# Four-layer attention and mixture-of-experts kernel: third expert stage with destinations inside the rows, next weights issued by ScalarE, and the last group of the third attention normed by VectorE

## What is computed

```python
x = x + _L0_xattn_ref(ctx_1024, _layernorm(x), ...); x = x + _L0_ffn_ref(_layernorm(x), ...)
x = x + _L1_xattn_ref(_layernorm(x), ctx_1024, ...); x = x + _L1_ffn_ref(_layernorm(x), ...)
x = x + _L2_xattn_ref(ctx_1024, _layernorm(x), ...); x = x + _L2_ffn_ref(_layernorm(x), ...)
x = x + _L3_xattn_ref(_layernorm(x), ctx_1024, ctx_1024, ...); x = x + _L3_ffn_ref(_layernorm(x), ...)
```

```python
def _L2_ffn_ref(x, gate_w, gate_up_w, down_w):
    router_probs = jax.nn.softmax(x_flat @ gate_w, axis=-1)
    top_k_probs, top_k_idx = jax.lax.top_k(router_probs, TOP_K)      # TOP_K = 2
    top_k_probs = top_k_probs / jnp.sum(top_k_probs, axis=-1, keepdims=True)
    gate_up = jnp.einsum('nd,edh->enh', x_flat, gate_up_w)
    hidden = jax.nn.silu(gate_up[..., :F]) * gate_up[..., F:]
    expert_out = jnp.einsum('enf,efd->end', hidden, down_w)
    ...   # each row takes the outputs of its two experts, weighted
```

## Time and profile before

| | |
|---|---|
| median of 3 runs | 1934.75 us (1924.11 to 1939.05) |
| profiled execution, its own time | 1931.34 us |
| its span, first to last instruction | 1929.6 us |
| mean granted TensorE clock | 0.854 |
| busy: PE, DVE, ACT, POOL | 77%, 61%, 43%, 40% of the span |
| third attention, its loop and what surrounds it | about 674 to 1479 us |
| third expert stage | about 1479 to 1634 us |

### The profile page before, as it was taken

The page is one execution under the profiler, slowest core; times in us unless marked ns, Lnnn a source line. Parts: engine busy times, 40 slices in busy tenths (PEclk is TensorE's granted clock), DMA queues, the critical chain, the costliest instruction groups (busy, mean ns, idle before and its releaser), DMA issues. The chain is left out here.

```text
span 1929.6 us, 36666 instructions
## 1 busy us (share of the span) xinstructions
PE 1489.4 (77%) x10502; PEld 1341.8 (70%) x10503; DVE 1176.5 (61%) x3742; ACT 821.3 (43%) x2527; POOL 777.7 (40%) x769
## 2 busy tenths in 40 slices
PE   6776999336576659999999999999983796463773
PEld 4555999225456549999999999999973685243773
DVE  4556444127866437778787878787863464767223
ACT  4443555102122136666666666666641222341331
POOL 2012442650001545555656556565543454001662
PEclk8776999655666769999999999999995898775986
DMA  9203222110012120000000000000002422102113
GB/s 188 1 0 116 76 65 55 49 41 1 1 44 73 36 88 12 12 2 15 10 16 7 15 7 18 4 7 4 11 8 74 123 73 73 56 1 61 42 41 105
DMA packets 90308, 78.57 MB, mean 41 GB/s; under 512 B 16196, under 2 KB 77351, under 8 KB 90087
## 3 DMA queue, kind: packets, MB, share of 16 engines
q1 hardware_dynamic: 71432, 49.20, 10.2%
q0 software_dynamic: 12160, 24.99, 4.3%
q10 hardware_dynamic: 6624, 3.28, 0.6%
HBM read 50.86 MB, written 27.10 MB: 40 GB/s over the span
## 5 line engine op out<-in xcount | busy, mean ns | idle before, releaser
L1800 POOL TENSOR_TENSOR paired_rows<-paired_rows,rinv 128x1024 f32<-128x1024 f32 x128 | 242.6, 1895 | 282.8 <-DVE rinv L2106 279.8
L1963 ACT ACTIVATE paired_rows<-psum_banks,neg_max 128x256 f32<-128x256 f32 x512 | 237.4, 490 | 0.6 <-DVE neg_max L2111 0.6
L2097 DVE TENSOR_TENSOR probs_turned_lo<-psum_banks,probs_turned_hi 128x512 fp32r<-128x512 f32 x256 | 175.7, 686 | 96.4 <-ACT probs_turned_hi L1945 82.5
L1851 PE MATMUL psum_banks<-y_turned_parts,queries_hi 128*128 128x256 f32 x1024 | 201.0, 294 | 3.0 <-DVEq L1701 3.0
L1886 PE MATMUL psum_banks<-probs_turned_hi,y_rows 128*128 128x512 f32 x512 | 192.0, 416 | 0.4 <-issue 0.4
L1945 ACT CAST probs_turned_hi<-psum_banks 128x512 fp32r<-128x512 f32 x256 | 151.1, 590 | 57.4 <-PE psum_banks L1835 55.0
L1835 PE MATMUL psum_banks<-ident,paired_rows 128*128 128x128 f32 x1024 | 155.4, 274 | 8.3 <-DVEq L1701 3.0
L1851 PEld LDWEIGHTS psum_banks<-y_turned_parts,queries_hi 128*128 128x128 f32 x1024 | 158.9, 192 | 3.5 <-issue 3.5
L2111 DVE TENSOR_REDUCE neg_max<-psum_banks 128x4 f32<-128x1024 f32 x128 | 156.0, 1219 | 7.1 <-PE psum_banks L1851 4.2
L1945 ACT CAST queries_hi<-psum_banks 128x512 fp32r<-128x512 f32 x128 | 75.0, 586 | 172.4 <-PE psum_banks L1874 169.1
L1851 PE MATMUL psum_banks<-y_turned_parts,queries_lo 128*128 128x256 f32 x512 | 145.0, 283 | 0.0
(11 more groups left out here) (747 smaller groups left out, 3465.3 us busy)
## 6 DMA issues: line engine op xcount, KB each, us to landing
normed_rows_dram<-paired_rows SPq DMA_DIRECT2D x3, 2048.0 KB, 8.7
tile_rows__<-rows_by_expert SPq DMA_DIRECT2D x71, 65.0 KB
expert_rows<-expert_rows_sb SPq DMA_DIRECT2D x71, 64.0 KB, 1.5
expert_w_b<-in_L_ffn_w_dram SPq DMA_DIRECT2D x2, 2048.0 KB
staged_pairs<-expert_rows SPq DMA_DIRECT2D x8, 512.0 KB
paired_rows<-expert_rows SPq DMA_DIRECT2D x8, 512.0 KB, 6.0
x_rows<-in_x_dram SPq DMA_DIRECT2D x8, 256.0 KB, 5.5
expert_w_a<-in_L_ffn_gate_up_w_dram SPq DMA_DIRECT2D x1, 2048.0 KB, 9.7
```

The costliest lines, as they stand in the source:

```text
L1800: ins = pool.tensor_tensor(probs[:, p, :, :], probs[:, p, :, :], rinv[:, p, :].unsqueeze(2).to_broadcast([P, 4, 256]), ALU.mult)
L1851: ins = pe.matmul(bank[S_BANKS[par] + h // 2][:, (h % 2) * 256:(h % 2 + 1) * 256], queries[q][:, h, :], yparts[:, 2 * s2 + y, :], start=(k ...
L1963: ins = act.activation(probs[:, par, h, :], bank[S_BANKS[par] + h // 2][:, (h % 2) * 256:(h % 2 + 1) * 256], ACT.Exp, bias=nmax[:, par, h: ...
L2097: ins = dve.tensor_tensor(lo, bank[bank_][:, :], hi.bitcast(F32), ALU.subtract)
```

## The change

- The rows in HBM are 129 words: 128 values and the destination itself, as an integer. For that each group's tail exists twice (`tails[0]`, `tails[1]`), one for each choice, with 2n and 2n+1 in the last word. ScalarE makes the second copy in `keep_tail`; the tiles lie in `Y1`, those of the last group in `XN`, no longer in `staged_pairs`.
- In the third expert stage VectorE no longer computes the destination; POOL's scatter reads it from the loaded tile. A tile load therefore waits until the slot's old tile has been scattered (`slot_is_free`).
- The fourth layer's weights are issued by ScalarE at the start of the third expert stage, before its table load and first Silu, and no longer by SP between the loads of tiles 7 and 8.
- The last group of the third attention: Ln and Exp on ScalarE, one refinement and the scalings on VectorE (four for each copy, the signal to TensorE after the first four). POOL no longer scales there. Its places have a buffer of their own.
- The paddings are split: experts 0 to 3 on SP's queue, 4 to 7 on ScalarE's. ScalarE's stand between `keep_tail` of the last group and the Exp for the mix weights.
- A table with Ln and Exp is loaded on ScalarE at the attention's start. The table of owners for all partitions goes; one partition's remains.

```diff
-        xb = nc.dram_tensor("rows_by_expert", [E * REGION + SPARE_TILES * P, P + 2], F32).ap()
+        xb = nc.dram_tensor("rows_by_expert", [E * REGION + SPARE_TILES * P, P + 1], F32).ap()
...
                     def load_tile(j, s):
                         if not isinstance(j, int) or j >= SLOTS:
-                            sp.wait_ge(rows_turned_kept.sem, j + (rows_turned_kept.value - SLOTS + 1))
+                            slot_is_free(sp, j, s)
...
-                    if layer in (0, 2):
+                    if layer == 0:
                         load_expert_weights(sp, layer + 1)
...
-                            pool.indirect_dma_start(ys, bass.IndirectOffsetOnAxis(ap=DEST[:, i:i + 1], axis=0), yo[:, i % SLOTS, :], None).then_inc(expert_out[i % SLOTS].sem, 16)
+                            to = xr[:, i % SLOTS, P:P + 1].bitcast(U32) if kept else DEST[:, i:i + 1]
+                            pool.indirect_dma_start(ys, bass.IndirectOffsetOnAxis(ap=to, axis=0), yo[:, i % SLOTS, :], None).then_inc(expert_out[i % SLOTS].sem, 16)
...
+                    if layer == 2:
+                        load_expert_weights(act, layer + 1)
                     run(act, step)
...
-                            if kept:
-                                dve.tensor_scalar(DEST[:, bass.ds(j, 1)], xr[:, s, P + 1:P + 2], tile_owner[:, bass.ds(j, 1)], xr[:, s, P:P + 1], ALU.not_equal, ALU.add)
                             dve.tensor_copy(xt[:, s % 2, :], bank[s % 2][:, 0:P]).then_inc(rows_turned_kept.sem, 1)
...
+                def place_pads(eng, experts_):
+                    eng.wait_ge(ends_known.sem, 1)
+                    for e in experts_:
+                        at_ = eng.value_load(pad_at[0:1, e:e + 1], min_val=0, max_val=E * REGION - P)
+                        eng.dma_start(xb[bass.ds(at_, P), :], pads_dram[e * P:(e + 1) * P, :]).then_inc(pads_placed.sem, 16)
...
-                            pool.indirect_dma_start(xb, bass.IndirectOffsetOnAxis(ap=spots[:, k, j:j + 1], axis=0), rows_of(n)[:, j, :], None).then_inc(rows_spread.sem, 16)
+                            pool.indirect_dma_start(xb, bass.IndirectOffsetOnAxis(ap=spots_of(n)[:, k, j:j + 1], axis=0), rows_of(n)[k][:, j, :], None).then_inc(rows_spread.sem, 16)
...
                     spread(NG - 2, range(2 * G))
-                    tail_part(NG - 1, 10)
                     spread(NG - 1, range(2 * G))
...
                 def keep_tail(act, n):
                     act.wait_ge(tail_turned_made.sem, n + 1)
+                    if not (isinstance(n, int) and n == NG - 1):
+                        act.copy(tails[1][:, :, 0:P], tails[0][:, :, 0:P])
                     act.copy(flat(tail_turned[:, :, :]), bank[Q_BANK][:, :]).then_inc(tail_kept.sem, 1)
...
-                        dve.tensor_scalar(rows_of(n)[:, :, P], row_number[:, bass.ds(n * G, G)], 2.0, None, ALU.mult)
-                        dve.tensor_copy(rows_of(n)[:, :, P + 1], ix[:, :, 0])
                         for k in range(2):
+                            dve.tensor_scalar(rows_of(n)[k].bitcast(U32)[:, :, P], row_number[:, bass.ds(n * G, G)], 2.0, float(k), ALU.mult, ALU.add)
...
                 @block.scalar
                 def _(act):
+                    act.preload_act_table_set("natural_log_exp_and_others")
                     keep_turned(act, 0, Q_BANK, context_turned, 0, 2)
...
                     all_steps(act_step)(act)
+                    act.wait_ge(spread_known.sem, spread_known.value + 1)
+                    act.activation(row_work[:, 2, G:2 * G], row_work[:, 0, G:2 * G], ACT.Ln, scale=-2.0)
+                    act.drain()
+                    act.activation(row_rstd[:, G:2 * G], row_work[:, 2, G:2 * G], ACT.Exp, scale=-0.5).then_inc(roots_made.sem, 1)
                     keep_tail(act, NG - 1)
+                    place_pads(act, range(E // 2, E))
                     act.wait_ge(leads_made.sem, 1)
...
                     aggregate(dve, ch, [1])
-                    seed(dve, ch)
-                    refine(dve, ch, 3)
-                    keep_scales(dve, ch, None, NG - 1)
+                    dve.tensor_scalar(row_work[:, 0, G:2 * G], row_mv[:, G:2 * G, 1], EPS, -0.5, ALU.add, ALU.mult).then_inc(spread_known.sem, 1)
+                    dve.wait_ge(roots_made.sem, roots_made.value + 1)
+                    refine(dve, ch, 1)
+                    for k in range(2):
+                        for j in range(G):
+                            ins = dve.tensor_scalar(last_tails[k][:, j, 0:P], x_tile(NG - 1)(j), row_mv[:, G + j, 0:1], row_rstd[:, G + j:G + j + 1], ALU.subtract, ALU.mult)
+                        if k == 0:
+                            ins.then_inc(tail_ready.sem, 1)
```

64 lines of the change are left out of this document (31 added, 33 removed).

## The result

| | before | changed |
|---|---|---|
| median of 20 runs | 1931.76 us | 1920.34 us |
| ratio of the changed kernel to before, with 95% interval | | 0.9946 (0.9930 to 0.9962) |
| profiled execution, its own time | 1931.34 us | 1927.02 us |
| its span, mean granted clock | 1929.6 us, 0.854 | 1925.3 us, 0.856 |

A forecast was written before the change was run, and what follows sets the result against it. It took TensorE to bound the attention loop, then an unfilled handover, a load-queue hole and late VectorE in the tile loop. Terms -9.0 - 9.2 - 9.0 + 3 - 1 = -25.2 took 1934.75 to 1909.5 us; range 1899 to 1926.

The forecast's parts named there:

- Handover: Third attention's end into the third expert stage: moving the scalings off POOL saves 9.0 us (7 to 10).
- Hole and half clock: Third expert stage's start: weights on ScalarE's queue remove TensorE's 9.76 us tile wait and 1.96 behind it, 11.7 us.
- Start: Third expert stage's first tiles: weights moving while they load cost 1.5 us (0 to 4.0).
- Slower release: Third expert stage: slots freed after the scatter instead of the turn cost 1.0 us at the start (0 to 2).
- The landing: Third expert stage: a scatter's data, with the signal, taken to land 1.5 us after its 0.97 us issue.
- Tile loop: Third expert stage: dropping VectorE's destination instruction saves 0.13 us a tile over 71 tiles, 9 us (0 to 16).
- nothing in the tile loop: Rival, third expert stage: the wait moves to ScalarE's gate and the start gives back more; 1924 us, chance 0.14.
- shut-out: Rival, third expert stage's start: weights block tile loads from either queue, costing 12 us; 1918.5 us, chance 0.28.
- Attention loop: Third attention: ScalarE's second copy makes TensorE wait 0.45 us in each of 7 groups, +3 us (0 to 4).
- Table: Third attention: preloading the table moves a 1.28 us load into idle time, -1 us (0 to 1.3).
- main path: Whole kernel: the queues share the DMA engines and all terms sum to 1909.5 us; chance 0.52.

The follow-up runs named there:

- weights_late: Changed kernel with the next layer's weights issued on ScalarE's queue behind the third tile's gate instead of ahead of the first; ratio to before 0.9964.
- dve_extra: Changed kernel with VectorE's old destination instruction put back in the third expert stage, its output not read, scatters kept; ratio to before 0.9948.
- weights_sp: Changed kernel with the next layer's weights back on SP's queue, behind the first eight tile loads; ratio to before 0.9967.

## Why the prediction was wrong

- *Handover, -9.0: right.* 2.61 us from the variance to the transposes. To SP's first load it is -10.3; that the rest comes from the paddings, which now end before POOL, is likely and not shown. Two blocks of spreads with 4.18 between, as written.
- *Hole and half clock, -11.7: right in size, wrong in reason, so the size was luck.* From the first to the eleventh tile 11.3 came back. But the step "If the two queues share the DMA engines freely, the 9.76 goes" failed. ScalarE's queue has the hole too if it is used at about the old moment (`weights_late`: TensorE waits 7.22, 9.99 from tile to tile; before 9.76 and 11.52). What took the hole away was that the weights now flow while the first tiles are on their way.
- *Start, +1.5: mis-sized, 4.6.* The bounds ended at 4.0, taken from the earlier trace rows, where the weights lay beside POOL's gathers, and 1.5 was taken because "later tiles are issued long before they are needed". But the first tile has nothing ahead of it. In eleven other runs with the weights issued first it took 6.5 to 7.6 us to the first tile, so it cost up to 5.6.
- *Slower release, +1.0: nothing, as long as no weights flow.* In `weights_late`, where they flow, a slow scatter delays the release; the runs don't say what share of the hole is due to that. The landing that the prediction had to guess (0.97 + 1.5) was about right: on the second kind it is 2.3 us from a scatter's issue in the median.
- *Tile loop, -9.0: wrong on the chips of the first kind, +1.1 (from the eleventh tile to the next block 123.6 to 127.1 us in seven profiles of this loop, 122.2 and 122.8 before, so 1 to 5 us more).* The failed step is reading: VectorE's wait ahead of the removed instruction was "issue", so VectorE was called the late one. `dve_extra` shows what that reading was worth: with the instruction back the time is the same (0.9948). What VectorE gave earlier, 0.2 us a pair, came back as a later signal: from the products to the late gate 1.35 us before, 1.54 now, the end pinned to POOL's scatter. The rival "nothing in the tile loop" had the right outcome, with ScalarE's gate as the place, and not the cause. It priced the whole at 1924, the start at its end; the result lies between it and the shut-out's 1918.5 (its own sum, 1934.75 - 16, gives 1918.75). Where signals are not late, on the second kind, the same edit is worth 0.07 us a tile, about half of the 0.13 taken.
- *Attention loop, +3: right,* 0.54 a group, 3.9 in all. *Table, -1:* -2.2.

Sum by the profile: -10.3 + 4.6 - 11.3 + 1.1 + 3.9 - 2.2 = -14.2, by the ratio -10.4 (7.3 to 13.5 less); the spread of the loop between profiles is enough for the difference. The measured 1920 lies inside the forecast's range, but the main path to 1909.5 was wrong. Of the 11 us that the profile's sum lies short of the forecast, the tile loop is 10.1 and the start 3.1. The shut-out rival (0.28) is half true: weights hold back what lies beside them from whatever queue they are issued, but they slow it, they don't shut it out: the first tile came after 6.6 us, not 15. On this the Trainium skill, "DMA: Bandwidth & Descriptors", section "Issuing engines are not separate DMA queues", is borne out by `weights_late` against `weights_sp` (0.9964 and 0.9967): with the weights at about the same moment, it made no difference from which engine they were issued.

## What to carry to other kernels

When a loop's slack is put down to one engine's "issue", compare two neighbouring turns of the loop first. Here the same instruction's consumer started 0.65 us after it in one and 1.55 in the next; the bound was a late signal, and an instruction taken from another engine gave nothing. The 4 MB of weights were paid for by whatever load was awaited beside them, from either queue; moved into the next stage, where nothing waited for them, they gave 4.8 us by the ratios. The copy put ahead of one that TensorE waits for cost nearly its own length (0.54 of 0.6 us a group) though the engine had idle time; behind it, it cost 0.1.

## What was not expected of the hardware

- On chips of the first kind ScalarE often gets TensorE's signal late when it falls due 0.4 to 1.0 us after the start of a POOL scatter (23 of 35 in the changed kernel): 0.56 us after the scatter's end in the median, so 0.7 (before) to 0.9 us (changed) later than the same signal otherwise. The Trainium skill, "SBUF — State Buffer", section "SBUF: two separate sides", has TensorE and ScalarE wait for no one, and on the engines' side contention between GpSimd and VectorE alone. That is told of data ports, and these runs don't show them to be touched; the signals are, and the page gives no word on them.
- On chips of the second kind the same kernel shows none (0 of 56, 0 of 62), and the kernel before takes 1825 to 1827 us and not 1932. Most of these 107 us lie far from the change, in the second attention, where POOL issues indirect gathers one behind the other. VectorE's reduction there waits for TensorE's products alone; first kind and second kind, changed kernel, POOL's gather shown with the first:

```profile
358.74 1.99 PE L1557 MATMUL psum_banks<-wsmall,u_rows___ 128*128 128x256 f32 x8
...
392.18 0.94 POOL L1281 DMA_INDIRECT paired_rows<-expert_rows,slots  x1 [0.30 <-issue]
392.30 0.69 DVE L1421 TENSOR_REDUCE head_sums___<-psum_banks 128x64 f32<-128x512 f32 x1 [30.90 <-remote]
```
```profile
357.40 1.99 PE L1557 MATMUL psum_banks<-wsmall,u_rows___ 128*128 128x256 f32 x8
359.43 0.69 DVE L1421 TENSOR_REDUCE head_sums___<-psum_banks 128x64 f32<-128x512 f32 x1 [0.45 <-PE psum_banks L1557]
```

  The reduction starts 31.57 us after the products' end on the first kind, 0.04 us after it on the second; the semaphore's update is recorded at 392.27 and 359.40. This wait and the two behind it make 64.3 to 66.7 us in all fourteen profiles of the first kind and are in none of the six of the second. So late signals are no matter of this loop alone, and POOL's gathers go on beyond 392 us, so the end of POOL's work is not what frees them there.
- Why the chips differ was not tried. All times here are of recorded executions, and whether recording has a share is not tested either: in 80 us of the changed kernel's loop 10 of VectorE's 44 updates for the turned tile have a record on the first kind, all 52 on the second, and without scatters all 49 on the first. The kind of chip decides what the change is worth: 10.4 us on one, 17.2 (ratio 0.9906) on the other, though the two intervals (0.9930 to 0.9962, 0.9875 to 0.9938) overlap a little.
- Two prices of a queue: a quiet tile load is at TensorE after 1.9 to 2.1 us, one beside the 4 MB of weights after 6.5 to 7.6, with POOL's scatter slower as well (`weights_late`: issued 1485.03, SP's wait for it over at 1491.24).
